# A graph layer whose last product is made of three f16 products instead of one f32 product

## The chip, the cores and the metric

The kernel runs on one core of one Trainium2 chip. The metric is the device time of one execution in microseconds (us); lower is better. The engines are called as the profile calls them: PE is TensorE (its weight loads are PEld), DVE is VectorE, ACT is ScalarE, POOL is GpSimd, SP is SyncE, which here only issues transfers.

## The reference, cut to what matters

A layer norm of 6250 nodes with 256 features goes into a two-layer graph convolution and a mixing block, whose sum with x is the `x` of the last lines. What the change touches is the last block, here without its zero or constant parts:

```python
x_mid = (x @ W_x + b_x).reshape(B, N, H, D).transpose(0, 2, 1, 3)          # H = 8, D = 64
slice_weights = softmax((x_mid @ W_slice + b_slice) / temp, axis=-1)       # N x 64 for each head
slice_token = einsum('bhnc,bhng->bhgc', fx_mid, slice_weights) / (slice_weights.sum(axis=2)[..., None] + 1e-05)
q, k, v = slice_token @ W_q, slice_token @ W_k, slice_token @ W_v
attn = softmax(einsum('bhgc,bhkc->bhgk', q, k) * D ** -0.5, axis=-1)
out_slice = einsum('bhgk,bhkc->bhgc', attn, v)                             # 64 tokens per head
out_x = einsum('bhgc,bhng->bhnc', out_slice, slice_weights)
return x + out_x.transpose(0, 2, 1, 3).reshape(B, N, INNER) @ W_out + b_out
```

The last two lines are one product in the kernel: the weights of a node (512 numbers, 8 heads of 64) times a fixed 512 x 256 matrix `pmat`, which is `out_slice` times `W_out` head by head.

## The kernel before, in words

The 6250 nodes are T = 49 tiles of 128 (the last has 106). The program has a long first part (edge lists, first graph layer), which the change leaves alone, and two stages that it touches. Each stage ends with a barrier of all engines. Within a stage every engine has a program of its own, written out by hand, and waits for others by semaphores; transfers go out in the order of the engine that issues them.

**The second graph layer** (the stage before the last). PE goes through the tiles; one tile is 49 steps `k` of four f16 products 128x128 (`sum_tile`, L1532), and pieces of work on earlier tiles are hung into the steps: at k = 3 `mix` of tile t-1 (L1551), at 6 `multiply` (L1541), at 31 `turn_x` (L1559), at 37 `logits` (L1568), and at 44 `weigh` of tile t-2 (L1578, which turns the softmax weights through the unit matrix, and L1584, which sums them with the features). Between them DVE does `norm` (L1616 to L1638), `shift`, `divide` and `split` (L1643 to L1668) of a tile, ACT does `rest` and `turned`, POOL three sums. `turned` (L1702) scales the turned weights out of PSUM into `wt` in f32 (512 numbers in each of 128 partitions), adds a store of them to `wT_dram`, and POOL adds `wt` to `w_acc`. At the end DVE and ACT each scale half of a sum of all tiles into `sT` (L1680, L1715), and ACT waits until the last stores have landed.

**The last stage.** SP loads the stored weights of all 49 tiles back, 256 KB each, into 36 slots (`turned_rows`; the first 24 are called `big` in rows, the next 12 `at`, then `big` again); from tile 36 on it waits until a slot has been used. Meanwhile a chain of small products and copies runs from `sT` to `pmat` (L1790 to L1853; PE, DVE and ACT take turns). Then PE makes the last product, four f32 products of 256 columns for each tile (L1830; the profile has two matmul rows for each f32 product), in four PSUM banks in turn; DVE adds the result to `x1` (L1909), and ACT issues the store of the 128 finished rows (L1856).

## Time and profile before

| what | us |
|---|---|
| median of 3 runs (lowest, highest) | 1991.46 (1989.37, 1993.24) |
| the profiled execution, its own time | 1991.08 |
| its span in the profile | 1989.2 |
| second graph layer, from about | 1053 |
| last stage, from | 1868.24 |
| last product (L1830), from and to | 1897.28, 1984.5 |

PE is busy for 94% of the span, DVE for 60%, ACT for 43%, POOL for 15%. Busy shares are means over stages with different limits, so each stage is looked at by itself. In the rows, a line such as `PE L1532 MATMUL ps<-at,big` gives the engine, the line of the kernel and the tiles written and read. In a timeline, several instructions of one group that follow each other are one row, with their count behind it, the time from the first start to the last end in front, and, in brackets, how long the engine had been idle and who released it.

### The profile page before, as it was taken

How to read it: one execution, taken by the hardware profiler on the slowest of the kernel's cores; microseconds unless marked ns; L12 is line 12 of the kernel's file. 1: busy time of each engine (PE TensorE's matmuls, PEld its weight loads, DVE VectorE, ACT ScalarE, POOL GpSimd, SP SyncE). 2: the span in 40 equal slices, each digit the busy share in tenths (PEclk: the TensorE clock that was granted, in tenths of full speed). 3: DMA queues.
4: the chain of work that ended last, by engine and by line, in shares of the span. 5: the costliest groups of instructions: out<-in, count | busy, mean ns of one | idle time of the engine just before them, and what ended most of it. 6: DMA issues, size and time to landing. Idle time of an engine off the chain costs nothing. (4 is left out here: it accounts for less than half of the span.)

```text
span 1989.2 us, 44436 instructions
## 1 busy us (share of the span) xinstructions
PE 1874.9 (94%) x18541; PEld 1380.8 (69%) x18541; DVE 1200.6 (60%) x2699; ACT 853.4 (43%) x1971; POOL 307.2 (15%) x417
## 2 busy tenths in 40 slices
PE   3599979999999999999979999999999999999699
PEld 3254545555555555555558888888888888888487
DVE  6899987666666666666505555555555555555422
ACT  1577765666566666666602222222222222222200
POOL 3143110000000000000011111111111111111100
PEclk7799989999999999999989999999999999999789
DMA  3133322222322223222253433333433344432462
GB/s 98 55 115 104 100 83 98 119 109 98 130 98 122 107 98 130 98 122 106 98 188 133 138 136 136 129 129 133 135 132 136 138 139 138 139 138 98 133 200 72
DMA packets 78659, 239.28 MB, mean 120 GB/s; under 512 B 12603, under 2 KB 45307, under 8 KB 65899
## 3 DMA queue, kind: packets, MB, share of 16 engines
q1 hardware_dynamic: 62205, 212.42, 29.7%
q10 hardware_dynamic: 14076, 19.25, 2.7%
q0 software_dynamic: 2176, 4.75, 0.9%
q8 instruction: 148, 2.42, 0.5%
q14 instruction: 54, 0.43, 0.1%
HBM read 125.59 MB, written 111.62 MB: 119 GB/s over the span
## 5 line engine op out<-in xcount | busy, mean ns | idle before, releaser
L1314 PE MATMUL ps<-hs,at 128*128 128x512 f16 x2401 | 668.5, 378 | 0.4 <-POOL at L1131 0.4
L1532 PEld LDWEIGHTS ps<-at,big 128*128 128x128 f16 x9604 | 556.4, 98 | 45.2 <-issue 8.9
L1532 PE MATMUL ps<-at,big 128*128 128x128 f16 x9604 | 577.5, 219 | 7.4 <-DMA at<-at_scratch 7.4
L1370 ACT CAST at<-ps 128x392 f16<-128x392 f32 x784 | 376.3, 488 | 286.8 <-PE ps L1275 271.5
L1275 PE MATMUL ps<-big 128*128 128x98 f16 x3136 | 471.1, 208 | 7.9 <-DVE big L1215 7.9
L1275 PEld LDWEIGHTS ps<-big 128*128 128x128 f16 x3136 | 297.4, 98 | 141.9 <-DVE big L1215 9.5
L1314 PEld LDWEIGHTS ps<-hs,at 128*128 128x128 f16 x2401 | 229.9, 97 | 148.7 <-issue 1.3
L1215 DVE TENSOR_TENSOR big<-iota_lo,key_lo 128x1024 f16<-128x1024 f16 x392 | 269.3, 687 | 0.0
L1215 DVE TENSOR_TENSOR big<-iota_hi,key_hi 128x784 f16<-128x784 f16 x392 | 219.8, 561 | 0.0
L1643 DVE SCALAR_TENSOR_TENSOR big<-ps,small,blogb 128x512 f32<-128x512 f32 x49 | 36.8, 751 | 230.2 <-PE ps L1568 230.2
L1747 POOL TENSOR_TENSOR key_lo<-key_lo,big 128x512 f32<-128x512 f32 (+1 forms) x49 | 62.0, 1265 | 663.0 <-ACT big L1702 663.0
L1226 DVE TENSOR_TENSOR big<-ps,big 128x256 f32<-128x256 f32 x49 | 20.8, 425 | 198.1 <-ACT big L1378 198.1
L1131 POOL TENSOR_TENSOR at<-at,ident 128x120 f16<-128x120 f16 x98 | 30.1, 319 | 660.4 <-ACT at L1370 660.4
L1691 ACT ACTIVATE big<-big,eps 128x1 f32<-128x1 f32 x49 | 14.6, 297 | 224.0 <-DVE big L1628 224.0
L1693 ACT CAST big<-ps 128x512 f16<-128x512 f32 x49 | 28.8, 587 | 170.7 <-PE ps L1559 170.7
L784 PE MATMUL ps<-at,big 128*128 128x512 f32 (+1 forms) x196 | 98.7, 627 | 0.0
L1695 ACT ACTIVATE big<-big 128x512 f32<-128x512 f32 x49 | 30.9, 631 | 146.8 <-DVE big L1649 146.8
L1616 DVE SCALAR_TENSOR_TENSOR big<-ps,dun,key_hi 128x256 f32<-128x256 f32 x49 | 23.7, 484 | 88.3 <-PE ps L1541 88.3
L1568 PE MATMUL ps<-wlog,big 128*128 128x512 f16 x294 | 72.7, 384 | 0.7 <-ACT big L1693 0.7
L1584 PE MATMUL ps<-big 128*128 128x512 f16 (+1 forms) x294 | 72.8, 384 | 0.0
L1659 DVE SCALAR_TENSOR_TENSOR big<-big 128x512 f32<-128x512 f32 x49 | 67.3, 1374 | 1.7
L1830 PE MATMUL ps<-big 128*128 128x256 f32 (+1 forms) x296 | 66.6, 389 | 0.7 <-ACT big L1853 0.7
(282 smaller groups left out, 2310.7 us busy)
## 6 DMA issues: line engine op xcount, KB each, us to landing
at_scratch<-at SPq DMA_DIRECT2D x49, 1568.0 KB, 5.1
at<-at_scratch SPq DMA_DIRECT2D x49, 1568.0 KB, 6.8
xT_scratch<-big SPq DMA_DIRECT2D x98, 128.0 KB, 1.7
big<-xT_scratch SPq DMA_DIRECT2D x49, 256.0 KB, 3.2
wT_scratch<-big ACTq DMA_DIRECT2D x49, 256.0 KB, 2.0
big<-in_x_dram SPq DMA_DIRECT2D x96, 128.0 KB, 2.5
big<-wT_scratch SPq DMA_DIRECT2D x37, 256.0 KB, 3.7
out_dram<-hs ACTq DMA_DIRECT2D x48, 128.0 KB
```

Of the source, the lines that this page charges most:

```text
L784: mm = te.matmul(ps[0:rows(t), 1 + b % 2, :], lhsT=xt_now[:, b, c, 0:rows(t)], rhs=wqk[:, c, :], start=False, stop=(c == CB - 1))
L1215: last = v.tensor_tensor(hot[:, s, :].rearrange("p (q k r) -> p q k r", k=width, r=2), iota.rearrange("p (o k) r -> p o k r", o=1).to_broa ...
L1275: te.matmul(ps[:, BANKS[i // UW % len(BANKS)], i % UW * KC:(i % UW + 1) * KC], lhsT=hot_lo[:, s, :].rearrange("p (q k r) -> p q k r", k=P, ...
L1314: mm = te.matmul(ps[:, 2 + b, :], lhsT=at[:, b, k * P:(k + 1) * P], rhs=hs[:, k, :], start=(k == 0), stop=(k == T - 1))
L1370: a.copy(to.rearrange("p k (i j) -> p k i j", j=WIN), ps[:, BANKS[m % len(BANKS)], 0:UW * KC].rearrange("p (i k j) -> p k i j", i=UW, j=WI ...
L1532: mm = te.matmul(ps[:, b, c * NT:(c + 1) * NT], lhsT=hs2[:, k, h * C + c * P:h * C + (c + 1) * P], rhs=at[:, b, k * P:(k + 1) * P], start= ...
L1568: mm = te.matmul(ps[0:NT, 4, :], lhsT=xn2T[:, b, xh, c * NT:(c + 1) * NT], rhs=wlog16[:, wh, c, :], start=(c == 0 and xh == wh == 0), stop ...
L1584: mm = te.matmul(ps[:, 6 + c, :], lhsT=x_half[0:rows(t), b, c * P:(c + 1) * P], rhs=w_half[0:rows(t), b, :], start=False, stop=False, skip ...
L1643: v.scalar_tensor_tensor(out=lg[0:NT, b].rearrange("p h d -> p (h d)"), in0=ps[0:NT, 4, :], scalar=unscale[0:NT], in1=blogb[0:NT, :], op0= ...
L1659: v.scalar_tensor_tensor(out=ew[0:NT, b], in0=ew[0:NT, b], scalar=WS, in1=hsum[0:NT, b, :].rearrange("p (h o) -> p h o", o=1) .to_broadcas ...
L1747: g.tensor_tensor(w_acc[:, :, 0:rows(t)], w_acc[:, :, 0:rows(t)], wt[:, b, :, 0:rows(t)], ALU.add).then_inc(w_added, 1)
L1830: mm = te.matmul(ps[0:rows(t), 4 + t % 4, 0:C], lhsT=turned_rows[t % SLOTS][:, p * NT:p * NT + rows(t)], rhs=pmat[:, p, :], start=(p == 0) ...
```

## The change

The turned weights are no longer stored in f32, but as two f16 halves that lie beside each other: `high = f16(2^15 w)` and `low = f16(2^15 w - high)`. Together they take as many bytes as the f32 numbers did. `pmat` is scaled by a power of two and split in the same manner; the last product is then high x high + low x high + high x low, in f16, and DVE scales it back as it adds it to `x1`. The power of two follows from the widest element of `vv` (the values `v`) and of `wfo` (`W_out`), which are found in the last stage.

`turned` of a tile moves from behind `rest` of the next tile to ahead of `rest` of the tile after that. DVE makes the low half at the start of its next tile, and the store is issued behind that.

```diff
+            wt16 = take([P, 2, 2, HB * NT], F16)
...
-        pmat = take([P, HB, C])
+        pmat = take([P, 2, HB, C], F16)
...
+                def low_turned(t, b):
+                    dve.wait_ge(wt_ready, 2 * t + 2)
+                    v.scalar_tensor_tensor(out=wt16[:, b, 1], in0=wt[:, b].rearrange("p a b -> p (a b)"), scalar=WS,
+                                           in1=wt16[:, b, 0], op0=ALU.mult, op1=ALU.subtract).then_inc(wt_low, 1)
+
                 def tile(t, b, u):
-                    if reached(t, 0):
+                    if reached(t, 2):
+                        low_turned(t - 2, b)
+                    if within(t, T):
                         norm(t, b, u)
                         shift(t, b)
                         divide(t, b)
                         split(t, b)
...
                     a.mul(wt[:, b].rearrange("p a b -> p (a b)"), ps[:, 5, 0:HB * NT], 1.0 / WS).then_inc(wt_ready, 1)
-                    act.wait_ge(wt_ready, t + 1)
+                    act.wait_ge(wt_ready, 2 * t + 1)
+                    a.mul(wt16[:, b, 0], wt[:, b].rearrange("p a b -> p (a b)"), WS).then_inc(wt_ready, 1)
+
+                def keep_turned(t, b):
+                    act.wait_ge(wt_low, t + 1)
                     act.dma_start(wT_dram[bass.ds(t, 1)].rearrange("t p n -> (t p) n"),
-                                  wt[:, b].rearrange("p a b -> p (a b)")).then_inc(w_out[b], 16)
+                                  wt16[:, b].rearrange("p a b -> p (a b)")).then_inc(w_out[b], 16)
 
                 def tile(t, b, u):
                     if within(t, T):
+                        keep_sums(t, b)
+                    if reached(t, 2):
+                        turned(t - 2, *shifted_slot(b, u, -2, 2))
+                    if within(t, T):
                         rest(t, b)
-                    if reached(t, 1):
-                        turned(t - 1, *shifted_slot(b, u, -1, 2))
-
-                pipeline(tile, T, 2, lag=1)
+                    if reached(t, 2):
+                        keep_turned(t - 2, b)
+
+                pipeline(tile, T, 2, lag=2)
...
-                pe.wait_ge(pmat_ready, 2)
+                pe.wait_ge(pmat_ready, 3)
                 for t in range(T):
                     pe.wait_ge(w_in[t % IN_SEMS], 16 * (t // IN_SEMS + 1))
                     if t >= 4:
                         pe.wait_ge(summed, t - 3)
-                    for p in range(HB):
-                        mm = te.matmul(ps[0:rows(t), 4 + t % 4, 0:C], lhsT=turned_rows[t % SLOTS][:, p * NT:p * NT + rows(t)],
-                                       rhs=pmat[:, p, :], start=(p == 0), stop=(p == HB - 1))
+                    for wh, mh in ((0, 0), (1, 0), (0, 1)):
+                        if t == 0 and mh == 1:
+                            pe.wait_ge(pmat_ready, 4)
+                        for p in range(HB):
+                            at_w16 = (wh * HB + p) * NT
+                            mm = te.matmul(ps[0:rows(t), 4 + t % 4, 0:C], lhsT=turned_rows[t % SLOTS][:, at_w16:at_w16 + rows(t)],
+                                           rhs=pmat[:, mh, p, :], start=(wh == mh == p == 0), stop=(mh == 1 and p == HB - 1))
                     mm.then_inc(mixed, 1)
...
-                act.wait_ge(pe_step, 8)
-                a.copy(pmat[:, 2:4].rearrange("p a b -> p (a b)"), ps[:, 3, :]).then_inc(pmat_ready, 1)
+                act.wait_ge(dve_step, 7)
+                for i in range(2):
+                    act.wait_ge(pe_step, 9 + i)
+                    a.activation(pmat[:, 0, 2 * i:2 * i + 2].rearrange("p a b -> p (a b)"), ps[:, 2 + i, :], ACT.Identity,
+                                 scale=small[:, 15:16]).then_inc(pmat_ready, 1)
...
+                v.tensor_reduce(small[:, 10:11], wfo.rearrange("p a b -> p (a b)"), AX.X, ALU.max, apply_absolute_value=True)
...
+                for i in range(2):
+                    dve.wait_ge(pmat_ready, 1 + i if i == 0 else 3)
+                    v.scalar_tensor_tensor(out=pmat[:, 1, 2 * i:2 * i + 2].rearrange("p a b -> p (a b)"), in0=ps[:, 2 + i, :],
+                                           scalar=small[:, 15:16], in1=pmat[:, 0, 2 * i:2 * i + 2].rearrange("p a b -> p (a b)"),
+                                           op0=ALU.mult, op1=ALU.subtract).then_inc(pmat_ready, 1)
                 for t in range(T):
                     dve.wait_ge(mixed, t + 1)
-                    v.tensor_tensor(x1[0:rows(t), t, :], ps[0:rows(t), 4 + t % 4, 0:C], x1[0:rows(t), t, :],
-                                    ALU.add).then_inc(summed, 1)
+                    v.scalar_tensor_tensor(out=x1[0:rows(t), t, :], in0=ps[0:rows(t), 4 + t % 4, 0:C],
+                                           scalar=small[0:rows(t), 16:17], in1=x1[0:rows(t), t, :],
+                                           op0=ALU.mult, op1=ALU.add).then_inc(summed, 1)
```

How this moves instructions is shown at three places. The first is ACT in the second graph layer, from one tile's sums to the next. In the lines of before, L1689 keeps the sums of a tile, L1691 to L1695 are the square root, a copy and the exponential of `rest`, and L1702 and L1704 are `turned` and its store. Before:

```order
L1689 COPY big<-ps 128x256 [waits l2_multiplied,l2_summed]
L1691 ACT_TABLE_LOAD
L1691 ACTIVATE big<-big,eps 128x1 [waits l2_ln_step]
L1693 CAST big<-ps 128x512 [waits xn2_turned]
L1695 ACT_TABLE_LOAD
L1695 ACTIVATE big<-big 128x512 [waits shifted]
L1702 ACTIVATE big<-ps 128x512 [waits w_added,w_out1,w_turned]
L1704 DMA wT_scratch<-big 128x512 [waits wt_ready]
```

Now, with L1712 and L1714 for the f32 weights and their high half, and L1718 for the store:

```order
L1697 COPY big<-ps 128x256 [waits l2_multiplied,l2_summed]
L1712 ACTIVATE big<-ps 128x512 [waits w_added,w_out0,w_turned]
L1714 ACTIVATE big<-big 128x512 [waits wt_ready]
L1701 ACT_TABLE_LOAD
L1701 ACTIVATE big<-big,eps 128x1 [waits l2_ln_step]
L1703 CAST big<-ps 128x512 [waits xn2_turned]
L1705 ACT_TABLE_LOAD
L1705 ACTIVATE big<-big 128x512 [waits shifted]
L1718 DMA wT_scratch<-big 128x1024 [waits wt_low]
```

`turned` has gone from the end of the tile to the place behind the sums, with one more operation, and the store stands at the end by itself. The number of table loads is the same, 99.

The second place is DVE in the same stage, where one tile's `split` (L1667 and L1669 now, L1666 and L1668 before) is followed by the next tile's `norm` (L1617, L1616 before).

```order
L1667 CAST big<-big 128x512 [waits soft_step]
L1669 TENSOR_TENSOR big<-big 128x512 [waits soft_step]
L1673 SCALAR_TENSOR_TENSOR big<-big 128x512 [waits wt_ready]
L1617 SCALAR_TENSOR_TENSOR big<-ps,dun,key_hi 128x256 [waits l2_multiplied]
L1621 TENSOR_TENSOR big<-ps,big 128x256 [waits l2_biased,l2_mixed]
```

L1673, the low half, stands where nothing stood.

The third place is the end of that stage and the chain of the last stage on ACT. L1733 is the scaling of `sT` (L1715 before); L1867 to L1880 are the chain's copies.

```order
L1712 ACTIVATE big<-ps 128x512 [waits w_added,w_out0,w_turned]
L1714 ACTIVATE big<-big 128x512 [waits wt_ready]
L1718 DMA wT_scratch<-big 128x1024 [waits wt_low]
L1733 ACTIVATE key_lo<-ps 128x512 [waits s_added]
L1471 UNCONDITIONAL_BRANCH [waits w_out1,w_out0]
L1859 UNCONDITIONAL_BRANCH [waits barrier_Pool_Activation_PE_DVE_SP_release]
L1867 COPY big<-ps 128x512 [waits f_pe_step]
L1869 ACTIVATE big<-ps 128x512 [waits f_pe_step]
L1870 COPY big<-ps 128x512
L1872 ACTIVATE big<-big 128x256 [waits f_dve_step]
L1874 COPY big<-ps 128x512 [waits f_pe_step]
L1876 COPY big<-ps 128x512 [waits f_pe_step]
```

The last store now stands behind an operation of ACT (L1714) and one of DVE (`wt_low`) more than before; in the chain the copies stand in the same order.

## Rows read from the trace of the kernel before

**Rows 1.** Busy time by stretches (us from the start): engines, granted clock, DMA share, GB/s
```profile
1200.00:1800.00 600.00, 600.00 (x8219) 531.97 (x8217) 339.05 (x638) 175.70 (x249) 114.86 (x108) 1.00 0.40 136
...
1901.00:1902.00 1.00, 1.00 (x4) 0.82 (x3) 0.42 (x1) 0.00 (x0) 0.00 (x0) 0.50 0.87 297
1902.00:1903.00 1.00, 1.00 (x6) 0.87 (x6) 0.00 (x0) 0.00 (x0) 0.00 (x0) 1.00 0.87 228
...
1910.00:1985.00 75.00, 74.46 (x346) 65.06 (x344) 18.69 (x44) 0.00 (x0) 0.00 (x0) 1.00 0.34 109
```

**Rows 2.** Timeline of the last product's start and end (start, us)
```profile
1897.28 6.89 PE L1830 MATMUL ps<-big 128*128 128x256 f32 x20 [0.68 <-ACT big L1853]
1901.10 0.42 DVE L1909 TENSOR_TENSOR hs<-ps,hs 128x256 f32<-128x256 f32 x1 [5.47 <-PE ps L1830]
1903.35 0.42 DVE L1909 TENSOR_TENSOR hs<-ps,hs 128x256 f32<-128x256 f32 x1 [1.82 <-PE ps L1830]
...
1984.50 0.42 DVE L1909 TENSOR_TENSOR hs<-ps,hs 106x256 f32<-106x256 f32 x1 [1.30 <-PE ps L1830]
```

**Rows 3.** Timeline of f16 products in one tile of the second graph layer
```profile
1529.31 5.79 PEld L1532 LDWEIGHTS ps<-at,big 128*128 128x128 f16 x100
1529.52 5.75 PE L1532 MATMUL ps<-at,big 128*128 128x128 f16 x100
```

**Rows 4.** Weight loads by line: count | busy us, mean ns | idle before
```profile
L1532 PEld LDWEIGHTS ps<-at,big 128*128 128x128 f16 x9604 | 556.4, 98 | 45.2 <-issue 8.9
```

**Rows 5.** Timeline of the same tile on ACT, DVE and PE
```profile
1525.46 0.37 ACT L1689 COPY big<-ps 128x256 f32<-128x256 f32 x1 [0.85 <-PE ps L1532]
...
1527.41 1.09 DVE L1668 TENSOR_TENSOR big<-big 128x512 f16<-128x512 f32 x1
...
1529.73 0.48 DVE L1616 SCALAR_TENSOR_TENSOR big<-ps,dun,key_hi 128x256 f32<-128x256 f32 x1 [1.22 <-PE ps L1541]
...
1531.71 0.30 ACT L1691 ACTIVATE big<-big,eps 128x1 f32<-128x1 f32 x1 [4.58 <-DVE big L1628]
...
1533.01 0.43 DVE L1638 TENSOR_TENSOR big<-big 128x256 f16<-128x256 f32 x1
1535.11 0.39 PE L1559 MATMUL ps<-ident,big 128*128 128x128 f16 x4
```

**Rows 6.** Line L1659: duration in ns, min/median/max, and starts
```profile
L1659 DVE SCALAR_TENSOR_TENSOR big<-big x49: 693/1389/1396, 1053.5 to 1860.8; 128x512 f32<-128x512 f32 x49
```

**Rows 7.** Timeline of the second graph layer's end, and its last stores
```profile
1863.04 0.69 DVE L1668 TENSOR_TENSOR big<-big 128x512 f16<-128x512 f32 x1
1863.79 0.89 PE L1578 MATMUL ps<-ident,big 106*128 106x106 f16 x8 [4.76 <-DVE big L1668]
1864.72 0.60 ACT L1702 ACTIVATE big<-ps 128x512 f32<-128x512 f32 x1 [4.46 <-PE ps L1578]
1867.28 0.69 DVE L1680 TENSOR_SCALAR key_lo<-ps 128x512 f32<-128x512 f32 x1 [3.54 <-PE ps L1584]
1868.24 3.23 SPq L1774 DMA_DIRECT2D big<-wT_scratch  x5
...
wT_scratch<-big ACTq DMA_DIRECT2D x2, 256.0 KB, 2.0
```

**Rows 8.** Chain that ended last, in the last stage (start, us)
```profile
1868.28 3.46 PE ps L1790 x16
...
1892.82 3.80 PE ps L1820 x8
...
1896.64 0.59 ACT big L1853
```

**Rows 9.** DVE by line and shape: operations nearest to the new ones
```profile
L1175 DVE TENSOR_REDUCE small<-wlog 128x1 f32<-128x1024 f32 x1 | 1.2, 1215 | 0.0
L1188 DVE TENSOR_SCALAR small<-small 128x1 f32<-128x1 f32 x1 | 0.2, 208 | 0.0
```

**Rows 10.** Timeline of SP's load issues, last row: the 13 behind the first 36
```profile
1901.09 21.56 SPq L1774 DMA_DIRECT2D big<-wT_scratch  x13
```

More of the change, by code:

```diff
@@ L1574, in weigh @@
                     if reached(t, 1):
-                        pe.wait_ge(wt_ready, t)
+                        pe.wait_ge(wt_ready, 2 * t - 1)
                     for p in range(HB):
@@ L1677, in _ @@
                 dve.wait_ge(w2_loaded, 32)
-                pipeline(tile, T, 2)
+                pipeline(tile, T, 2, lag=2)
                 dve.wait_ge(s_added, T)
@@ L1684, in _, with keep_sums @@
                 a = nc.scalar
-                def rest(t, b):
+                def keep_sums(t, b):
                     act.wait_ge(summed, t + 1)
@@ L1689, in rest @@
                     a.copy(aggT[:, b].rearrange("p a b -> p (a b)"), ps[:, b, 0:CB * NT]).then_inc(aggT_ready, 1)
+                def rest(t, b):
                     act.wait_ge(ln_step, 2 * t + 2)
@@ L1702, in turned @@
                     a.mul(wt[:, b].rearrange("p a b -> p (a b)"), ps[:, 5, 0:HB * NT], 1.0 / WS).then_inc(wt_ready, 1)
-                    act.wait_ge(wt_ready, t + 1)
+                    act.wait_ge(wt_ready, 2 * t + 1)
+                    a.mul(wt16[:, b, 0], wt[:, b].rearrange("p a b -> p (a b)"), WS).then_inc(wt_ready, 1)
+                def keep_turned(t, b):
+                    act.wait_ge(wt_low, t + 1)
                     act.dma_start(wT_dram[bass.ds(t, 1)].rearrange("t p n -> (t p) n"),
-                                  wt[:, b].rearrange("p a b -> p (a b)")).then_inc(w_out[b], 16)
+                                  wt16[:, b].rearrange("p a b -> p (a b)")).then_inc(w_out[b], 16)
                 def tile(t, b, u):
                     if within(t, T):
+                        keep_sums(t, b)
+                    if reached(t, 2):
+                        turned(t - 2, *shifted_slot(b, u, -2, 2))
+                    if within(t, T):
                         rest(t, b)
-                    if reached(t, 1):
-                        turned(t - 1, *shifted_slot(b, u, -1, 2))
-                pipeline(tile, T, 2, lag=1)
+                    if reached(t, 2):
+                        keep_turned(t - 2, b)
+                pipeline(tile, T, 2, lag=2)
                 act.wait_ge(s_added, T)
@@ L1721, in _ @@
                 g = nc.gpsimd
-                g.memset(w_acc, 0.0).then_inc(acc_ready, 1)
-                for z in (bdq, bdk, bdv):
+                for z in (w_acc, bdq, bdk, bdv):
                     last = g.memset(z, 0.0)
@@ L1781, in _ @@
                     last = g.memset(z, 0.0)
-                last.then_inc(cleared, 1)
+                last.then_inc(zeroed, 1)
             @block.tensor
@@ L1809, in _ @@
                 mm.then_inc(pe_step, 1)
-                pe.wait_ge(dve_step, 4)
+                pe.wait_ge(dve_step, 3)
+                te.transpose(peaks, small[:, 9:11], ident[:, :]).then_inc(pe_step, 1)
+                pe.wait_ge(dve_step, 5)
                 for p in range(HB):
@@ L1813, in _ @@
                 mm.then_inc(pe_step, 1)
+                pe.wait_ge(dve_step, 6)
+                te.matmul(peak_row, lhsT=ones_row, rhs=peak[:, 2:4], start=True, stop=True).then_inc(pe_step, 1)
                 pe.wait_ge(act_step, 4)
@@ L1874, in _ @@
                 dve.wait_ge(loaded, 160)
-                dve.wait_ge(cleared, 1)
+                dve.wait_ge(zeroed, 2)
                 for p in range(HB):
@@ L1888, in _ @@
                 v.tensor_copy(kT.rearrange("p a b -> p (a b)"), ps[:, 5, :]).then_inc(dve_step, 1)
+                dve.wait_ge(act_step, 2)
+                v.tensor_reduce(small[:, 9:10], vv.rearrange("p a b -> p (a b)"), AX.X, ALU.max, apply_absolute_value=True).then_inc(dve_step, 1)
                 dve.wait_ge(pe_step, 4)
@@ L1904, in _ @@
                 last.then_inc(dve_step, 1)
-                dve.wait_ge(pe_step, 7)
-                v.tensor_copy(pmat[:, 0:2].rearrange("p a b -> p (a b)"), ps[:, 2, :]).then_inc(pmat_ready, 1)
+                dve.wait_ge(pe_step, 5)
+                step(v.tensor_reduce(peak[:, 0:1], peaks, AX.X, ALU.max))
+                v.tensor_scalar(peak[:, 2:4], ident[0:2, 0:2], peak[:, 0:1], None, ALU.mult).then_inc(dve_step, 1)
+                dve.wait_ge(pe_step, 8)
+                step(v.tensor_copy(small[:, 11:13], peak_row))
@@ new lines, in _ @@
+                step(v.tensor_scalar(small[:, 13:14], small[:, 11:12], small[:, 12:13], float(D), ALU.mult, ALU.mult))
+                step(v.tensor_scalar(small[:, 13:14], small[:, 13:14], 1e-30, None, ALU.max))
+                v.tensor_scalar(small[:, 14:15].bitcast(I32), small[:, 13:14].bitcast(I32), EXPONENT, None, ALU.bitwise_and)
+                step(v.tensor_scalar(small[:, 15:16].bitcast(I32), small[:, 13:14].bitcast(I32), EXPONENT, EXPONENT,
+                                     ALU.bitwise_and, ALU.bitwise_xor))
@@ new lines, in _ @@
+                v.tensor_scalar(small[:, 16:17], small[:, 14:15], 2.0 ** -14 / WS, None, ALU.mult)
+                v.tensor_scalar(small[:, 15:16], small[:, 15:16], 2.0 ** 13, None, ALU.mult).then_inc(dve_step, 1)
+                dve.wait_ge(dve_step, 7)
+                for i in range(2):
[3 more added lines that the diff above has]
+                                           op0=ALU.mult, op1=ALU.subtract).then_inc(pmat_ready, 1)
```

19 lines of the change are left out of this document (10 added, 9 removed).

## The prediction

> **What bounds the kernel now.** I read the stretches first [rows 1]. In the middle of the second graph layer PE is busy for 600.00 of 600 us at full granted clock, while DVE has 339 us of work, ACT 176 and POOL 115: there PE sets the pace, and work added to the others is free until it makes PE wait. In the last product PE is again without a gap, and the row of 1910 to 1985 shows DVE at 18.7 of 75 us and the transfers at 0.34: PE bounds there too. So I ask of each edit whether it lies in one of these two PE-bound stretches, or in the two short pieces between them, the end of the graph layer and the chain to `pmat`, where engines wait for one another and each added microsecond counts.
>
> The timeline of the last product [rows 2] gives its shape. It starts at 1897.28; the first tile reaches DVE 3.82 us later, the second 2.25 us after that, and the other 47 take 1984.50 - 1903.35 = 81.15 us, or 1.727 us each. The start is slow because the granted clock is 0.50 (1.2 GHz) until about 1902 and 1.00 (2.4 GHz) from then on [rows 1]. I put the change at 1901.8, which fits the 2.25 us of the second tile: 4.5 us of product at the low clock.
>
> **The gain: the last product.** In f32 one tile is four products of 256 columns, eight rows in the trace, so 1.727 / 8 = 216 ns for each row. 512 columns at 2.4 GHz are 213.3 ns, so a row streams 512 columns, and 2.5 ns come on top. In f16 I look at the products of the graph layer, each with a weight load of its own: 100 of 128 columns start at 1529.52 [rows 3], and the next group starts at 1535.11 [rows 5], so 55.9 ns each, 53.3 of them columns, again 2.5 ns on top. A f16 product of 256 columns lies between the two in length: 106.7 + 2.5 = 109.2 ns, and twelve of them 1.310 us for a tile instead of 1.727.
>
> Weight loads have a mean of 98 ns [rows 4], nearly as long as a 109 ns product, so it matters whether they are hidden. In rows 3 a hundred loads take 5.79 us beside a hundred products in 5.75 us; 98 + 53 ns in turn would make 15 us. So loads run beside products there, even at half the column count.
>
> The Trainium skill, "TensorE: Matmul & The Clock Gate", section "Measured speedup vs the span model", says otherwise: a weight load overlaps products in flight only when it goes to another row group, which a 128 x 128 load can't. By that rule each of the twelve products would cost its load as well, 98 + 109 = 207 ns, a tile 2.49 us, and the change would lose; rows 3 contradict it, and the same page speaks elsewhere of loads pulled ahead into a background buffer. I go by the rows.
>
> With the clock rising 4.5 us into the product as now: at 1.2 GHz a f16 tile takes 12 x 256 / 1.2 = 2.56 us, so 1.76 tiles pass in 4.5 us; the other 47.24 take 61.9 us; the pipeline's fill, 3.82 us less the 3.41 us that eight times 512 columns take at 1.2 GHz, adds 0.4. Sum 66.8 us, against 1984.50 - 1897.28 = 87.2 us now. **Gain 20.4 us.** Bounds: full clock from the start 64.6 us (2.2 more gained); low clock for 9 us 69.0 us (2.2 less); 4 us less gained if a product takes 116 ns in place of 109. DVE's sum becomes an operation with a scalar from PSUM, 128x256; the nearest row, L1616, takes 0.48 us [rows 5], well under 1.31. What follows the last product (one DVE sum, the last store) stays.
>
> **The graph layer's loop: nothing.** ACT gets one operation per tile and DVE one. DVE: between `split` (L1668, ends 1527.41 + 1.09 = 1528.50) and `norm` (L1616, 1529.73) it is idle for 1.22 us, waiting for PE [rows 5]. The new low half, two SBUF inputs of 512, has L1659 as its nearest row: 0.69 us in the best tile and 1.39 in the median, when POOL works on SBUF beside it [rows 6]. So between 0.53 us of idle left and 0.17 us late. Behind `norm` there is more cover: its last step ends at 1533.44 and PE takes the result up at 1535.11, 1.67 us later. DVE would have to be 2.9 us longer before PE waits. On ACT, `turned` now runs behind the sums (1525.83) for 0.60 us [rows 7] plus about 0.6 for the high half, so until some 1527.1; then come the root's table load and the root, wanted at 1531.71, before which ACT idles 4.58 us now [rows 5]. POOL's sum over `w_acc` follows `turned` by some 2.4 us; what it delays (the next tile's bias) is wanted a tile later. The store, still 256 KB, goes out after the exponential, and its buffer is wanted again a tile later.
>
> **The graph layer's end: 1.5 us lost.** Now [rows 7]: `split` of the last tile ends at 1863.73, PE has turned it by 1864.68, L1702 scales it until 1865.32, and its store lands 2.0 us after issue, near 1867.4, hidden behind the sums' scaling, which ends last at 1867.97; the next stage starts at 1868.24. After: ACT first waits for the low half of the tile before (DVE, behind `split`: 1864.45), issues its store (about 0.3 us), then scales the last tile until 1865.4, makes the high half until 1866.05; DVE needs 0.69 to 1.39 us for the low half; the store then takes its 2.0: 1868.75 to 1869.45. That is 0.8 to 1.5 us behind 1867.97; I take 1.2. One tile earlier the low half also stands ahead of the last tile's `norm`, in a stretch where DVE has no slack any more: 0 to 0.7 us, I take 0.3.
>
> **The chain to `pmat`: 0.1 us.** The maximum over `wfo` (128x1024, 1.2 us by L1175 [rows 9]) stands ahead of the reciprocal on DVE, covered by PE's first products (1868.28, 3.46 us [rows 8]; DVE's own work there, L1870 to L1872, ends near 1869.5 now and near 1870.7 then). That over `vv` falls into the scores' products, the small transposes and the 2-row product into waits for ACT. The seven small operations that make the scale run while PE makes `pmat` (1892.82, 3.80 us [rows 8]): 7 x 0.21 us [rows 9] is 1.5 us. Then ACT writes the first high half, DVE its low half, and ACT the second high half when L1853 now copies the same bank (1896.64). PE starts there as now; the last low half, 0.7 us on DVE, is wanted after eight products, at 1.2 GHz 1.7 us. Bounds: 0 if all is covered, 1.0 if one copy of 0.6 us and some small steps come onto the path.
>
> **Sum.** 1991.08 (the profiled execution; span 1989.2 and 1.9 around it) - 20.4 + 1.2 + 0.3 + 0.1 = 1972.3. The median of the runs is 0.4 above the profiled one, so 1972.7 us, 0.9% faster. Runs of this kernel differ by 0.2% (4 us), about what can be told from no change.
>
> **Rivals.**
> - *Weight loads don't hide behind products of 256 columns* (the other side: slower). 98 + 109 ns for each product make 2.49 us per tile, about 122 us for 49, so 35 us more than now: 2008. It is the case that the Trainium skill's rule above describes. It decides from (87.2 - 1.6) / 49 = 1.75 us per tile, 146 ns a product. Against it: rows 3. For it: loads of 98 ns fill 90% of 109 ns, which leaves little room should they run one behind another. Chance 0.03; that they show in part (120 to 135 ns, 6 to 15 us of the gain gone, 1979 to 1988) 0.03.
> - *The loop stretches.* If the new order on ACT and DVE made PE wait by 0.2 us in each of 47 tiles, 9.4 us would go: 1982; at 0.4 us all the gain. For it: DVE's own idle of 1.22 us is nearly eaten. Against: 1.67 us behind it, and 4.58 on ACT. Chance 0.05, of it 0.01 slower than before.
> - *Transfers bound the last product.* A tile would want 256 KB in and 128 KB out in 1.31 us, 300 GB/s, as much as the 297 GB/s of the busiest row [rows 1]. But 36 of 49 loads are issued by the time the product has begun, and the last 13 follow used slots [rows 10], 47 us before they are wanted. All 19.3 MB at 297 GB/s are 65 us from about 1870, near 1935, and the product ends near 1966. If the loads did bind I put it at 1975 to 1980. Chance 0.03.
>
> **How the numbers follow.** Forecast 0.86, with its own range from the bounds of its terms: 1969 (clock up at once, end cheap) to 1978 (clock late, 1 us of chain, dear end, 2 us of slower products). Outside it on the slow side lie 0.03 + 0.03 + 0.05 + part of 0.03; so 1968.5 to 1978.5 leaves out less than 2 in 10. Faster by over 0.2%: forecast 0.86, transfers 0.03, loop 0.04, part-hidden loads 0.02, or 0.95; within 0.2% 0.01; slower 0.04.
>
> **What would show it.** In the new profile: rows of 128x256 f16 in the last product, DVE's sums 1.31 us apart, 65 to 69 us from first product to last sum; no idle time of PE in the loop, with DVE's idle ahead of `norm` near or under 0.5; the last stage starting 1 to 2 us later; PE's last product starting 29 us behind that as now. Wrong would be a spacing above 1.4 us, PE idle ahead of the turning that L1559 does now, or a DVE scale chain that ends after the second half of `pmat`.

## The result, and the profile after

The changed kernel takes 1971.87 us in the median of 3 runs (1971.09 to 1974.36), against 1991.46 before: a ratio of 0.9903, with a 95% interval of 0.9889 to 0.9918. That is 19.6 us less, where 18.8 were forecast, and the time lies inside the range. The execution that was profiled is the slowest of the three, 1974.36 us, with a span of 1972.6.

Both traces can be cut at the same four events: ACT's first copy of the second graph layer, SP's first load of the last stage, the first instruction of the last product, and DVE's last sum.

| piece, us | before | after | difference |
|---|---|---|---|
| start to ACT's first copy of the graph layer | 1036.96 | 1038.12 | +1.16 |
| graph layer, from there to the last stage's first load | 831.28 | 833.35 | +2.07 |
| chain, to the start of the last product | 29.04 | 29.60 | +0.56 |
| last product, to the start of the last sum | 87.22 | 66.70 | -20.52 |
| rest of the span | 4.7 | 4.8 | +0.1 |

The first piece is not touched by the change. Over the eleven traces of before, after and the experiments cut in this way it lies between 1036.0 and 1040.0 us, so its 1.16 us are scatter between executions, and the pieces behind it are compared each by itself. (PE's first products of the layer, L1532, start at 1023.69 us in before, so the layer begins earlier than the 1053 of the table of before.)

The last product first, in PE's and DVE's timelines, with the stretches under it (start, us; then, for the stretches, busy us of PE, PEld, DVE, ACT and POOL, the granted clock, the transfers' share and GB/s):

```profile
1900.33 0.69 ACT L1880 ACTIVATE big<-ps,small 128x512 f16<-128x512 f32 x1 [0.96 <-PE ps L1841]
...
1901.07 33.91 PE L1855 MATMUL ps<-big 128*128 128x256 f16 x288 [0.78 <-ACT big L1880]
...
1903.85 0.48 DVE L1957 SCALAR_TENSOR_TENSOR hs<-ps,small,hs 128x256 f32<-128x256 f32 x1 [2.05 <-PE ps L1855]
1906.20 0.48 DVE L1957 SCALAR_TENSOR_TENSOR hs<-ps,small,hs 128x256 f32<-128x256 f32 x1 [1.87 <-PE ps L1855]
1907.52 0.48 DVE L1957 SCALAR_TENSOR_TENSOR hs<-ps,small,hs 128x256 f32<-128x256 f32 x1 [0.83 <-PE ps L1855]
...
1967.77 0.48 DVE L1957 SCALAR_TENSOR_TENSOR hs<-ps,small,hs 106x256 f32<-106x256 f32 x1 [0.82 <-PE ps L1855]
```

```profile
1200.00:1800.00 600.00, 600.00 (x8216) 531.58 (x8215) 343.66 (x674) 199.09 (x286) 122.55 (x107) 1.00 0.40 135
1904.00:1905.00 1.00, 1.00 (x7) 0.72 (x5) 0.33 (x1) 0.00 (x0) 0.00 (x0) 0.50 0.78 258
1905.00:1906.00 1.00, 1.00 (x7) 0.73 (x6) 0.00 (x0) 0.00 (x0) 0.00 (x0) 0.59 1.01 353
...
1910.00:1965.00 55.00, 55.00 (x506) 49.30 (x505) 20.31 (x42) 0.00 (x0) 0.00 (x0) 1.00 0.47 152
```

The rows answer to [rows 1, 2]. The sums reach DVE 2.35 us apart at first and then 1.310 us: (1967.77 - 1906.20) / 47. PE is busy for 55.00 of 55 us, weight loads for 49.30 beside it, and DVE waits 0.82 us for PE in each tile, so PE is still the bound. The clock is 0.50 until some 1905.8 (0.59 is the mean over a microsecond in whose last fifth it is up), 4.7 us into the product as before.

In the middle of the graph layer PE is busy for 600.00 of 600 us at full clock, as it was; DVE has 4.6 us more work there, ACT 23.4 and POOL 7.7. One tile of it, in the timeline of DVE and POOL:

```profile
1510.10 0.43 DVE L1667 CAST big<-big 128x512 f16<-128x512 f32 x1
...
1510.56 0.69 DVE L1669 TENSOR_TENSOR big<-big 128x512 f16<-128x512 f32 x1
...
1510.66 1.71 POOL L1763 TENSOR_TENSOR key_lo<-key_lo,big 128x512 f32<-128x512 f32 x1 [13.38 <-ACT big L1712]
...
1511.28 1.64 DVE L1673 SCALAR_TENSOR_TENSOR big<-big 128x512 f16<-128x512 f32 x1
...
1513.98 0.48 DVE L1617 SCALAR_TENSOR_TENSOR big<-ps,dun,key_hi 128x256 f32<-128x256 f32 x1 [1.06 <-PE ps L1542]
```

The new low half (L1673) takes 1.64 us, more than its bound of 0.69 to 1.39, and yet DVE is idle for 1.06 us ahead of `norm` (L1617), nearly the 1.22 of [rows 5]. The durations by line of this operation and of one of the softmax's last steps tell why (ns, min/median/max):

```profile
L1660 DVE SCALAR_TENSOR_TENSOR big<-big x49: 691/692/1380, 1054.7 to 1862.6; 128x512 f32<-128x512 f32 x49
L1673 DVE SCALAR_TENSOR_TENSOR big<-big x49: 684/1645/1653, 1071.8 to 1868.0; 128x512 f16<-128x512 f32 x49
```

L1660 is L1659 of before, whose median was 1389 ns [rows 6]. It is 692 now; L1669 fell from 1.09 [rows 5] to 0.69, and L1667 from 0.83 to 0.43. In the timeline of before, POOL's sums ran beside just these three:

```profile
1524.69 1.27 POOL L1747 TENSOR_TENSOR key_lo<-key_lo,big 128x512 f32<-128x512 f32 x1 [13.64 <-ACT big L1702]
...
1525.12 1.39 DVE L1659 SCALAR_TENSOR_TENSOR big<-big 128x512 f32<-128x512 f32 x1
...
1526.04 1.05 POOL L1742 TENSOR_TENSOR big<-big,bvo 128x256 f32<-128x256 f32 x1
...
1526.54 0.84 DVE L1666 CAST big<-big 128x512 f16<-128x512 f32 x1
...
1527.05 0.91 POOL L1745 TENSOR_TENSOR hs<-hs,big 128x256 f32<-128x256 f32 x1
```

POOL's sum over `w_acc` (L1747, now L1763) follows `turned`, which moved, and its two shorter sums stand behind it. So they no longer run beside the softmax's last steps, and the sum over `w_acc` runs beside the low half and slows that one instead. The new work cost DVE little because an old cost went elsewhere.

### The profile page after: what moved, and what is told of

The parts are those of the page before. It is cut to its first block and busy times, and to the rows that moved or that the text cites. A ratio compares the mean times of both kernels' runs of the same rounds, so it can differ in the third digit from the quotient of the medians.

```text
span 1972.6 us, 44947 instructions
## 1 busy us (share of the span) xinstructions
PE 1857.7 (94%) x18740; PEld 1365.1 (69%) x18740; DVE 1215.8 (62%) x2760; ACT 883.3 (45%) x2021; POOL 319.0 (16%) x417
## 3 DMA queue, kind: packets, MB, share of 16 engines
q8 instruction: 150, 2.46, 0.5%
## 5 line engine op out<-in xcount | busy, mean ns | idle before, releaser
L1763 POOL TENSOR_TENSOR key_lo<-key_lo,big 128x512 f32<-128x512 f32 (+1 forms) x49 | 82.8, 1690 | 651.3 <-ACT big L1712 651.3
L1673 DVE SCALAR_TENSOR_TENSOR big<-big 128x512 f16<-128x512 f32 x49 | 79.0, 1613 | 3.2 <-ACT big L1714 1.8
L1617 DVE SCALAR_TENSOR_TENSOR big<-ps,dun,key_hi 128x256 f32<-128x256 f32 x49 | 23.7, 484 | 81.6 <-PE ps L1542 81.6
```

Of the source, the lines that this page charges most:

```text
L1673: v.scalar_tensor_tensor(out=wt16[:, b, 1], in0=wt[:, b].rearrange("p a b -> p (a b)"), scalar=WS, in1=wt16[:, b, 0], op0=ALU.mult, op1=AL ...
L1763: g.tensor_tensor(w_acc[:, :, 0:rows(t)], w_acc[:, :, 0:rows(t)], wt[:, b, :, 0:rows(t)], ALU.add).then_inc(w_added, 1)
```

## The experiments

Every run is compared with the kernel before on the same chip, whose medians lay between 1991.2 and 1991.9 us.

**The changed kernel once more**, for the scatter. No edit.

> The changed kernel once more. My theory: 1972 us within 2; in the profile the last product takes 66.7 us again, the end of the graph layer 2.1 us more than before, the chain 0 to 0.6 us more; what lies ahead of the graph layer may differ by 1 us either way between two executions of the same program. Rival (the 1.2 us that the first profile shows ahead of the graph layer belong to the change): they are there again.

1972.26 us (1971.88 to 1973.45), ratio 0.9908 [0.9891, 0.9924]. Its pieces against before: graph layer 833.11 (+1.83), chain 29.76 (+0.72), last product 66.86 (-20.36), +0.10 behind it, and -0.95 ahead of the layer. So from one execution to the next the pieces of the change stand within 0.3 us, and the 1.16 us ahead of the layer don't belong to the change. The chain's 0.72 is a little over the expected 0 to 0.6; what moves it is shown further down.

**The loop alone.** Everything up to the last stage is that of after, but the f32 weights are stored, and the last stage is that of before. Against after:

```diff
                     act.dma_start(wT_dram[bass.ds(t, 1)].rearrange("t p n -> (t p) n"),
-                                  wt16[:, b].rearrange("p a b -> p (a b)")).then_inc(w_out[b], 16)
+                                  wt[:, b].rearrange("p a b -> p (a b)")).then_inc(w_out[b], 16)
...
-                    for wh, mh in ((0, 0), (1, 0), (0, 1)):
-                        if t == 0 and mh == 1:
-                            pe.wait_ge(pmat_ready, 4)
...
+                    for p in range(HB):
+                        mm = te.matmul(ps[0:rows(t), 4 + t % 4, 0:C], lhsT=turned_rows[t % SLOTS][:, p * NT:p * NT + rows(t)],
+                                       rhs=pmat[:, p, :], start=(p == 0), stop=(p == HB - 1))
```

> Only the change's part in the graph layer (both halves are made, POOL, ACT and DVE in the new order), but the f32 weights are stored, behind the low half, and the last stage is that of before. My theory: the loop costs nothing and its end 2.1 us, so 1993.6 us against 1991.5, PE's period in the loop unchanged. Rival (the loop does stretch, and the last product gains more than it seems): 1997 us or more.

1991.7 us (1989.88 to 1993.87), ratio 1.0001 [0.9992, 1.0011]: the expected 2.1 us more is a miss in the times, which don't show the cost of the layer's end. The trace does: the layer takes 833.13 us, 1.85 more than before. Its product took 84.91 us in place of 87.22, which hides that in the profiled execution. A stretch of it, and the product's row in the chain that ended last:

```profile
1900.00:1901.00 1.00, 1.00 (x6) 0.87 (x6) 0.00 (x0) 0.00 (x0) 0.00 (x0) 1.00 0.98 338
```

```profile
1899.76 84.89 PE ps L1846 x392
```

The clock had its full level from the product's first microsecond on, where before had the lower one for 4.7 us [rows 1]. So the cost of 1.85 us is shown by the trace, and no time confirms it.

**Two products instead of three**, high x low left out, so that the low half of `pmat` isn't used: is PE still the bound?

```diff
-                    for wh, mh in ((0, 0), (1, 0), (0, 1)):
-                        if t == 0 and mh == 1:
+                    for wh, mh in ((0, 0), (1, 0)):
+                        if t == 0 and wh == 1:
                             pe.wait_ge(pmat_ready, 4)
...
-                                           rhs=pmat[:, mh, p, :], start=(wh == mh == p == 0), stop=(mh == 1 and p == HB - 1))
+                                           rhs=pmat[:, mh, p, :], start=(wh == mh == p == 0), stop=(wh == 1 and p == HB - 1))
```

> Leaves out the third product (high weights by the low half of pmat), so 8 products per tile instead of 12; all transfers stay. My theory (PE alone sets the pace, 109.2 ns a product): 0.874 us per tile, about 46 us for the last product instead of 66.7, 21 us less than the changed kernel: 1951 us. Rival (transfers bound the last product): no faster than 1.2 us per tile, at most 5 us less.

1950.15 us (1949.49 to 1952.52), ratio 0.9794 [0.9778, 0.9811].

A stretch of its last product, and two of DVE's sums in the timeline:

```profile
1910.00:1945.00 35.00, 35.00 (x323) 31.41 (x321) 19.34 (x40) 0.00 (x0) 0.00 (x0) 1.00 0.72 252
```

```profile
1931.04 0.48 DVE L1957 SCALAR_TENSOR_TENSOR hs<-ps,small,hs 128x256 f32<-128x256 f32 x1 [0.39 <-PE ps L1855]
1931.91 0.48 DVE L1957 SCALAR_TENSOR_TENSOR hs<-ps,small,hs 128x256 f32<-128x256 f32 x1 [0.39 <-PE ps L1855]
```

A tile takes 0.873 us, 8 x 109.2 ns, and the last product 44.93 us, 21.8 less than in after. PE has no gap, and the transfers move 252 GB/s at a share of 0.72 without holding it up. So neither transfers nor DVE were near to binding at three products, and one third of the product is worth its third.

**Half the columns for each product**, twice as many products and weight loads, the same result. If loads hid in part only, this would make them bind.

```diff
-                            mm = te.matmul(ps[0:rows(t), 4 + t % 4, 0:C], lhsT=turned_rows[t % SLOTS][:, at_w16:at_w16 + rows(t)],
-                                           rhs=pmat[:, mh, p, :], start=(wh == mh == p == 0), stop=(mh == 1 and p == HB - 1))
+                            for c in range(CB):
+                                mm = te.matmul(ps[0:rows(t), 4 + t % 4, c * P:(c + 1) * P],
+                                               lhsT=turned_rows[t % SLOTS][:, at_w16:at_w16 + rows(t)],
+                                               rhs=pmat[:, mh, p, c * P:(c + 1) * P], start=(wh == mh == p == c == 0),
+                                               stop=(mh == 1 and p == HB - 1), skip_group_check=True)
```

> Each f16 product of the last stage in two of 128 columns, each with its own weight load: 24 loads and 24 products per tile. My theory (loads run beside products, 55.9 ns each as in the graph layer): 1.342 us per tile in place of 1.310, 1.5 us more than the changed kernel: 1973.4 us. Rival (a load of 98 ns fills most of a 109 ns product and begins to show when products are shorter): 98 ns or more each, 2.35 us per tile, 45 us or more on top: 2017 us.

1972.88 us (1970.05 to 1974.2), ratio 0.9907 [0.989, 0.9925]: twelve more loads a tile can't be seen in the time.

The same two views of this kernel:

```profile
1910.00:1960.00 50.00, 50.00 (x900) 50.00 (x897) 18.19 (x38) 0.00 (x0) 0.00 (x0) 1.00 0.47 156
```

```profile
1931.26 0.48 DVE L1960 SCALAR_TENSOR_TENSOR hs<-ps,small,hs 128x256 f32<-128x256 f32 x1 [0.86 <-PE ps L1856]
1932.60 0.48 DVE L1960 SCALAR_TENSOR_TENSOR hs<-ps,small,hs 128x256 f32<-128x256 f32 x1 [0.86 <-PE ps L1856]
```

A tile takes 1.340 us in place of 1.310, which is 55.8 ns for each of 24 products. So each product costs its columns and 2.5 ns, and a load of 98 ns for every 55.8 ns costs nothing: the loads overlap one another as well, since 897 of them at 98 ns would fill 88 us and stand in 50. The Trainium skill, "TensorE: Matmul & The Clock Gate", section "The mechanism", has a load overlap products in flight only for another row group (the rule that the prediction weighed, which names the section behind this one for it). These loads fill all rows, and the trace doesn't agree: by that rule a tile here would take at least 24 loads and 24 products in turn, an estimate of 3.7 us.

**The low half twice, and six times**: how much more DVE work until PE waits? Each repeat writes the same numbers again; ACT's store waits for the last. The edit is that of two; six has 6 for each 2.

```diff
+                LOWS = 2
...
+                    for i in range(LOWS):
+                        if i > 0:
+                            dve.wait_ge(wt_low, LOWS * t + i)
+                        v.scalar_tensor_tensor(out=wt16[:, b, 1], in0=wt[:, b].rearrange("p a b -> p (a b)"), scalar=WS,
+                                               in1=wt16[:, b, 0], op0=ALU.mult, op1=ALU.subtract).then_inc(wt_low, 1)
...
-                    act.wait_ge(wt_low, t + 1)
+                    act.wait_ge(wt_low, 2 * (t + 1))
```

> DVE makes each tile's low half twice, one behind the other (the second changes nothing in the result). My theory (behind the low half DVE has 1.06 us of idle time left, and behind norm PE takes 1.6 us until it wants the result): the second one takes 0.7 to 1.4 us, DVE's idle time ahead of norm falls to 0 to 0.4 us, PE's period in the graph layer stays the same, only its end grows, by 1.5 to 2.5 us: 1974 us. Rival (the loop is at its edge): each tile 0.5 us longer or more, 1995 us or more.

> DVE makes each tile's low half six times. My theory: the five more take some 4.1 us, 3.1 us past DVE's idle time, 1.5 us past PE's cover, so the period grows from 16.90 to between 17.9 and 18.8 us, and the time by 45 to 90 us: 2015 to 2060 us. Rival (DVE has far more room, its share of 57% in the loop counts): less than 10 us more.

Twice: 1976.34 us. Six times: 2065.89 us. Each is a single run. From the timelines of DVE in the middle of the layer, of two low halves and then of six, of six PE's timeline too, and last a row of six's waits of PE (us in all, times, longest):

```profile
1613.31 2.78 DVE L1678 SCALAR_TENSOR_TENSOR big<-big 128x512 f16<-128x512 f32 x2
1616.01 0.48 DVE L1617 SCALAR_TENSOR_TENSOR big<-ps,dun,key_hi 128x256 f32<-128x256 f32 x1
```

```profile
1600.42 0.48 DVE L1617 SCALAR_TENSOR_TENSOR big<-ps,dun,key_hi 128x256 f32<-128x256 f32 x1
...
1604.19 0.40 PE L1560 MATMUL ps<-ident,big 128*128 128x128 f16 x4 [1.52 <-DVE big L1639]
...
1613.02 6.09 DVE L1678 SCALAR_TENSOR_TENSOR big<-big 128x512 f16<-128x512 f32 x6
1619.03 0.48 DVE L1617 SCALAR_TENSOR_TENSOR big<-ps,dun,key_hi 128x256 f32<-128x256 f32 x1
```

```profile
PE ps L1560 <- DVE big L1639: 58.1, 38, 1.8
```

With two (first fence) `norm` follows the low halves at once, so DVE's idle is used up, and PE doesn't wait anywhere between 1100 and 1800 us: the layer grows by 2.6 us against after (835.92; 1.5 to 2.5 were expected), at its end, where each tile's work stands in a row. With six (the other two) the period of a tile grows from 16.90 to 18.61 us (1619.03 - 1600.42) and PE waits at the turning, 38 times between 1100 and 1800 us, which is every tile at that period, 58.1 us in all. That is the wait which the rival of the stretched loop describes; it comes between two and six low halves. At six the period is inside the expected 17.9 to 18.8 us, and the time is above the expected 2015 to 2060. One low half more than the change has is what uses up DVE's own idle.

**POOL's sum behind the low half** instead of beside it.

```diff
-                        pool.wait_ge(wt_ready, 2 * t + 1)
+                        pool.wait_ge(wt_low, t + 1)
```

> POOL's sum over w_acc waits for the low half instead of the f32 weights, so that it starts behind DVE's low half instead of beside it. My theory (POOL's sum beside it is what makes the low half 1.64 us long): the low half falls to 0.69 us, POOL's sum from 1.7 to 1.3, DVE's idle time ahead of norm rises from 1.06 to 2.0 us, PE's period stays; the end of the graph layer is 0.5 to 1.0 us shorter: 1971 us against the changed kernel's 1972. Rival (the low half is slow in itself, through its f16 operand): it stays at 1.6 us.

The line of the low half (ns, min/median/max), and `norm` in the timeline:

```profile
L1673 DVE SCALAR_TENSOR_TENSOR big<-big x49: 682/693/924, 1073.1 to 1867.5; 128x512 f16<-128x512 f32 x49
```

```profile
1616.72 0.48 DVE L1617 SCALAR_TENSOR_TENSOR big<-ps,dun,key_hi 128x256 f32<-128x256 f32 x1 [2.01 <-PE ps L1542]
```

The low half falls from 1.645 to 0.693 us, POOL's sum from 1.712 to 1.267, and DVE's idle grows to 2.01 us: it was the two engines on SBUF at once that made both dearer. The layer takes 831.46 us, 1.9 less than after (0.5 to 1.0 were expected) and 0.17 more than before. Of the 1.9, 0.48 are `norm` of the last tile starting earlier; 1.09 are its L1660 and L1667, no longer beside POOL (0.69 and 0.43 us for 1.38 and 0.83). The time, 1972.86 us, ratio 0.9903 [0.9887, 0.992], can't tell 1.9 us.

**The turning at its old place**: `turned` behind `rest`, as before, but with its high half.

```diff
                     if within(t, T):
                         keep_sums(t, b)
-                    if reached(t, 2):
-                        turned(t - 2, *shifted_slot(b, u, -2, 2))
                     if within(t, T):
                         rest(t, b)
                     if reached(t, 2):
                         keep_turned(t - 2, b)
+                    if reached(t, 1) and within(t, T + 1):
+                        turned(t - 1, *shifted_slot(b, u, -1, 2))
```

> Undoes one part: turned (now with both operations of ACT) stands behind the exponential of the next tile again, as before the change; the low half and the store stay where the change put them. My theory: DVE's L1660, L1667 and L1669 are slow again (1.39, 0.83 and 1.09 us, beside POOL's sum), the low half takes 0.7 to 1.0 us, DVE's idle time ahead of norm is 0.2 to 0.6 us, PE's period stays the same, and the time is that of the changed kernel within 1 us: 1972. Rival (the move is what keeps the loop free): PE waits in each tile, 1980 us or more.

1971.97 us (1970.52 to 1973.56), ratio 0.9902 [0.9885, 0.9918]. POOL's sums go back with it: L1660 takes 1.39 us again, L1669 1.10, and the low half 0.68, as DVE's timeline of one tile has it:

```profile
1611.65 1.10 DVE L1669 TENSOR_TENSOR big<-big 128x512 f16<-128x512 f32 x1
1612.67 0.68 DVE L1673 SCALAR_TENSOR_TENSOR big<-big 128x512 f16<-128x512 f32 x1
1613.98 0.48 DVE L1617 SCALAR_TENSOR_TENSOR big<-ps,dun,key_hi 128x256 f32<-128x256 f32 x1 [0.62 <-PE ps L1542]
```

DVE keeps 0.62 us of idle, 0.44 less than in after, PE doesn't wait, and the layer takes 833.18 us for the 833.35 of after. So the move of `turned` is neutral; the gain is the f16 product's alone.

**Both halves straight from PSUM**, in search of a better version: ACT copies the high half from the bank, DVE takes the low half from the bank too, the store leaves at once, and the f32 weights for POOL come last.

```diff
-                        pe.wait_ge(wt_ready, 2 * t - 1)
+                        pe.wait_ge(wt_ready, 2 * t)
...
-                    v.scalar_tensor_tensor(out=wt16[:, b, 1], in0=wt[:, b].rearrange("p a b -> p (a b)"), scalar=WS,
-                                           in1=wt16[:, b, 0], op0=ALU.mult, op1=ALU.subtract).then_inc(wt_low, 1)
...
+                    v.tensor_tensor(wt16[:, b, 1], ps[:, 5, 0:HB * NT], wt16[:, b, 0], ALU.subtract).then_inc(wt_low, 1)
...
-                    a.mul(wt[:, b].rearrange("p a b -> p (a b)"), ps[:, 5, 0:HB * NT], 1.0 / WS).then_inc(wt_ready, 1)
-                    act.wait_ge(wt_ready, 2 * t + 1)
-                    a.mul(wt16[:, b, 0], wt[:, b].rearrange("p a b -> p (a b)"), WS).then_inc(wt_ready, 1)
...
+                    a.copy(wt16[:, b, 0], ps[:, 5, 0:HB * NT]).then_inc(wt_ready, 1)
...
+                    a.mul(wt[:, b].rearrange("p a b -> p (a b)"), ps[:, 5, 0:HB * NT], 1.0 / WS).then_inc(wt_ready, 1)
...
-                        pool.wait_ge(wt_ready, 2 * t + 1)
+                        pool.wait_ge(wt_ready, 2 * t + 2)
```

> A shorter end of the graph layer: ACT writes the high half straight from PSUM, DVE the low half from PSUM too, ACT issues the store at once and makes the f32 weights for POOL only behind it. My theory: the low half takes 0.7 us, PE's period in the loop stays at 16.90 us, and from the first tile's sums to the last stage's start pass 830.6 us, against 833.4 in the changed kernel and 831.3 before; the time falls by 2 to 3 us to 1969.5, at the edge of what the times can show. Rival (the end is bound by the sums' scaling, not by the store): no less than 831.3 us. Second rival (ACT now waits for DVE in each tile and PE waits for ACT): the period grows, 1975 us or more.

1973.78 us (1971.83 to 1976.75), ratio 0.9913 [0.9899, 0.9926]. A miss: the layer takes 833.98 us, 0.6 more than after, where 2.8 less were expected. The timeline of its end:

```profile
1850.81 1.26 POOL L1757 TENSOR_TENSOR key_lo<-key_lo,big 128x512 f32<-128x512 f32 x1 [13.95 <-ACT big L1715]
1851.10 1.26 DVE L1623 SCALAR_TENSOR_TENSOR hs<-big 128x256 f32<-128x256 f32 x1
...
1865.44 0.60 ACT L1715 ACTIVATE big<-ps 128x512 f32<-128x512 f32 x1 [3.40 <-DVE big L1673]
...
1866.18 0.86 PE L1579 MATMUL ps<-ident,big 106*128 106x106 f16 x8 [5.78 <-ACT big L1715]
```

The low half itself is cheap (0.68 us in the loop, 2.13 us of DVE idle), and the second rival falls too, since PE doesn't wait between 1100 and 1800 us. But the bank is now held until ACT has read it a second time (L1715), and PE may write the next turned tile into it only then: in the loop that is hidden, and at the end PE's last turning stands behind it. POOL's sum moved once more, beside L1623 of `norm`, which takes 1.26 us in place of 0.43 just where DVE has no slack.

## Why the prediction was right, step by step

**The last product: right.** Forecast 66.8 us, measured 66.70 and 66.86. The spacing of 1.310 us is the forecast one to the nanosecond, and the 4.7 us at the low clock stand for the 4.5 assumed. The rate taken from the graph layer's f16 products [rows 3], columns and 2.5 ns, holds at 256 columns, and `half_columns` shows it again at 128. That the size came out to 0.1 us is in part luck: the 4.5 us at the low clock were taken over from before, and in `turned_back`, with the same product, the clock was up 1.1 us ahead of it and the product took 64.40 us, near the bound of 64.6 that the prediction gives for that case.

**Rival of the weight loads: fallen.** `half_columns` doubles the loads, they fill the engine's whole time, and nothing is added but 12 x 2.5 ns a tile. The prediction's price for this rival doesn't follow from its own terms: 122 us for the product are 35 more than the 87.2 of before, so some 2028 us with the 1.6 of the end and the chain, where it says 2008, which is 35 over its forecast. The rival's chance doesn't hang on it.

**Rival of the transfers: fallen.** At two products the same bytes go through in two thirds of the time, with no gap of PE.

**The loop at nothing: right, by another sum.** PE's 600.00 of 600 us stand. The low half was sized at 0.69 to 1.39 us and took 1.64, outside the bounds, and DVE's idle ahead of `norm` was to be near or under 0.5 and is 1.06. The prediction has POOL's sum over `w_acc` follow `turned` and asks who waits for it; what it missed is whom POOL works beside: its sums left L1660, L1667 and L1669 (0.70, 0.41 and 0.40 us cheaper), and that over `w_acc` came to the low half. `pool_late` and `turned_back` show both ends of that: without POOL beside it the low half takes 0.69. The cover behind was sound: two low halves still cost no time of PE, six do.

**The graph layer's end: mechanism right, size off.** Forecast 1.5 us, measured 2.07 and 1.83. The term for the low half ahead of the last `norm` was 0.3, with a bound of 0.7. `norm` starts 812.82 us after the layer's first copy and started 812.34 after it: 0.48 late, since the low half took 1.64 us there as well. By the end of `split` that has grown to 0.70, four turning products (L1560) taking 0.61 us in place of 0.40 at a lower granted clock. From the end of `split` to the next stage it is 5.88 us and was 4.51: 1.37 for the forecast 1.2. The timeline of that piece:

```profile
1866.67 0.60 ACT L1712 ACTIVATE big<-ps 128x512 f32<-128x512 f32 x1 [3.90 <-PE ps L1579]
...
1867.30 0.63 ACT L1714 ACTIVATE big<-big 128x512 f16<-128x512 f32 x1
...
1867.96 1.02 DVE L1673 SCALAR_TENSOR_TENSOR big<-big 128x512 f16<-128x512 f32 x1 [1.77 <-ACT big L1714]
...
1869.01 0.33 ACTq L1718 DMA_DIRECT2D wT_scratch<-big  x1
...
1871.47 0.80 SPq L1791 DMA_DIRECT2D big<-wT_scratch  x2
```

Against [rows 7], the scaling of the last tile is followed by the high half (0.63), the low half (1.02) and then the store, after which the stage starts 2.46 us later, all of it in turn as forecast. In `pool_late` that piece is still 5.78 us; what it saves lies ahead of it: `norm` isn't late (812.35), and `split` ends 1.8 us earlier than in after, since the low half ahead of `norm`, L1660 and L1667 no longer run beside POOL.

**The chain: right, and what it grew by is the clock.** Forecast 0.1 us, measured 0.56 and 0.72. On the chain that ended last, only one row of the change shows: the scaled copy L1880, 0.69 us for the 0.59 of [rows 8]. From that chain (start, us, instructions), in after and then in before:

```profile
1871.50 3.76 PE ps L1807 x16
...
1884.36 1.43 PE ps L1820 x8
...
1900.33 0.69 ACT big L1880
```

```profile
1880.82 1.30 PE ps L1803 x8
```

Much of the rest are PE's own products: L1807 takes 3.76 us for 3.46 in [rows 8], and L1820 1.43 for the 1.30 of L1803, the same products before. Whether that is the clock can be read from two pairs of traces in which it rises and falls at the same places of the chain, within 0.2 us. The first of each pair has the old chain, the second the new one: before and `pool_late`, `loop_only` and `turned_back`. Their chains as stretches, in this order (columns as with the result, the granted clock third from the end):

```profile
1868.24:1897.28 29.04, 17.75 (x72) 14.86 (x72) 8.73 (x25) 3.84 (x7) 0.99 (x2) 0.68 0.86 276
```

```profile
1870.89:1899.92 29.03, 18.26 (x76) 15.23 (x76) 12.00 (x37) 4.62 (x8) 0.98 (x2) 0.68 0.83 266
```

```profile
1870.21:1899.76 29.55, 18.26 (x72) 15.39 (x72) 8.73 (x25) 3.83 (x7) 0.98 (x2) 0.58 0.86 274
```

```profile
1869.86:1899.54 29.68, 18.91 (x75) 15.89 (x76) 11.99 (x37) 4.62 (x8) 0.98 (x2) 0.58 0.84 270
```

At the same clock the new chain takes 29.03 us for 29.04, and 29.68 for 29.55: the edits cost nothing to 0.13 us, as forecast. The old chain by itself takes 0.51 us more at a granted clock of 0.58 than at 0.68, and its first products take the same 3.76 us in `loop_only` as the new chain's in after. Over all traces the new chain took 27.9 to 29.8 us. The maxima, the small transposes and the seven small operations don't appear on the chain that ended last: they were covered, as forecast.

**The sum.** In the profiled executions the pieces from the graph layer on give -20.52 + 2.07 + 0.56 + 0.07 = -17.8 us, where the forecast was -18.8: the layer's end cost 0.6 more than its terms, and the clock in the chain 0.5. The median of the runs fell by 19.6, and runs scatter by more than the difference; that the forecast time was met within 0.8 us is closer than its pieces were, and so in part luck.

## What to carry to other kernels

Where PE has no gap, count its columns: an f32 product of 256 columns cost 432 ns and three f16 products of halves 328 ns, and weight loads were free down to 128 columns. Where an operation is moved, look at who follows it on other engines: POOL's sums went with `turned` and made one DVE operation 0.95 us dearer and three others 1.5 us cheaper, so their price belongs to the place and not to the operation. The two halves, free in the pipelined loop, were paid for in the last tiles: 1.8 to 2.1 us. And a chain of short products is compared at the same granted clock, or its difference of half a microsecond is put down to the wrong cause.

## What the runs showed of the hardware that was not expected

DVE and POOL on SBUF at once. The low half took 0.69 us alone and 1.64 beside POOL's sum, the sum 1.27 alone, or when it started first as in before, and 1.71 when L1669 had started ahead of it; in `from_psum` L1623 took 0.43 alone and 1.26 beside it. The Trainium skill, "SBUF — State Buffer", section "Who interferes with whom", says that a DVE operation with two SBUF inputs contends with a POOL operation that reads SBUF, and that the later one stands still until the other is done. By that, as an estimate for the tile shown with the result, POOL's sum starts at 1510.66, stands until L1669 ends at 1511.25, and ends 1.27 later, at 1512.52; the low half then ends 0.69 behind it. The trace has 1512.37 and 1512.92, within 0.3 us of that, so it agrees but for that. The difference is regular: in the rows shown, L1659 and L1666 of before, L1673 of after and L1623 of `from_psum` end 0.55, 0.29, 0.55 and 0.29 us behind the end of the POOL sum that had started ahead of them, each 0.14 us less than the 0.69 or 0.43 that it takes alone. L1666 is a cast with a single SBUF input, and behaves like the others.

The clock at the start of the product. In nine of eleven traces PE made `pmat` at a granted clock of 0.50 (1.2 GHz) to its end, and the clock rose 3.9 to 5.1 us into the product. In `loop_only` and `turned_back` it rose some 1 us ahead of it, and the product was 2.3 us shorter (84.91 for 87.22, 64.40 for 66.70). The engine's work ahead of it was of the same kind, a chain of short products with waits between them; why the rise comes earlier in these was not settled.
